# A graph network on one core: sorting the edges by block prefix counts and spreading the record scatters over later stages

## The reference

```python
h = relu(layernorm(x)); x = x + gat(relu(gat(h, W1, ...)), W2, ...)          # 0a and 0b: attention by dst
h = relu(layernorm(x)); x = x + dot_attention(h, Wq, Wk, Wv)                 # 1: by dst
h = relu(layernorm(x)); x = x + layernorm(segment_sum(
        silu(concat(h[src], edge_attr_64) @ W + b), dst))                    # 2: by dst, uses the edge attributes
h = relu(layernorm(x)); x = x + relu(segment_softmax_sum(h @ W, src, dst))   # 3: by src
```

## Time and profile before

| | us |
|---|---|
| median of 3 runs | 8227.57 (8222.74 to 8235.5) |
| the profiled execution | 8211.48 |
| its span | 8209.5 |
| setup | 86.2 |
| histogram | 142.3 |
| ranking | 1039.9 |
| units "d" | 107.4 |
| dense and scores 0a, 0b, 1, 2 | 446.3 together |
| dense and scores 3 | 119.7 |
| the four finish stages | 146.7 together |

### The profile page before, as it was taken

The page is one execution under the profiler, slowest core; times in us unless marked ns, Lnnn a source line. Parts: engine busy times, 40 slices in busy tenths (PEclk is TensorE's granted clock), DMA queues, the critical chain, the costliest instruction groups (busy, mean ns, idle before and its releaser), DMA issues. The chain is left out here.

```text
span 8209.5 us, 130687 instructions
## 1 busy us (share of the span) xinstructions
PE 5150.4 (63%) x21517; PEld 3732.5 (45%) x21518; DVE 5912.1 (72%) x16005; ACT 3435.3 (42%) x8014; POOL 4715.1 (57%) x4888
## 2 busy tenths in 40 slices
PE   1445551347777547777456767766688885577775
PEld 1344441235555335555344545544566663344443
DVE  4877774557777757777758888888566667577777
ACT  0122220057777347777324444443233331266664
POOL 0477773067777157777235555553477773377774
PEclk9999999998888668888788888887899997577777
DMA  4233332145455145555245555554344442254453
GB/s 157 76 102 102 104 104 49 46 127 135 135 135 135 34 121 135 135 135 134 45 136 166 166 166 166 166 166 117 97 128 128 128 128 63 82 135 135 135 135 93
DMA packets 608540, 981.03 MB, mean 119 GB/s; under 512 B 315833, under 2 KB 370550, under 8 KB 608026
## 3 DMA queue, kind: packets, MB, share of 16 engines
q0 software_dynamic: 248160, 655.67, 29.8%
q1 hardware_dynamic: 359898, 299.06, 12.8%
q10 hardware_dynamic: 416, 25.60, 0.9%
HBM read 945.69 MB, written 60.94 MB: 123 GB/s over the span
## 5 line engine op out<-in xcount | busy, mean ns | idle before, releaser
L1488 POOL DMA_INDIRECT ad_ring<-tab_qv,ad_idx x816 | 774.1, 949 | 946.6 <-PE ad_po L1690 278.2
L458 POOL DMA_INDIRECT recs_s<-plc_recr,plc_posu x784 | 774.3, 988 | 528.6 <-DVE plc_ohl L405 289.9
L1028 POOL DMA_INDIRECT at_ring<-tab_s,at_idx x816 | 784.0, 961 | 468.0 <-DVE acc L1041 216.0
L1028 POOL DMA_INDIRECT at_ring_0b<-tab_s,at_idx_0b x816 | 784.2, 961 | 455.7 <-issue 206.1
L1028 POOL DMA_INDIRECT at_ring_0a<-tab_s,at_idx_0a x816 | 784.9, 962 | 444.4 <-issue 210.0
L1879 POOL DMA_INDIRECT ae_ring<-tab_a,ae_idx x816 | 795.6, 975 | 397.0 <-issue 232.2
L438 PE MATMUL plc_got<-plc_base_sb,plc_lot 128*128 128x25 f32 x1568 | 488.4, 399 | 501.5 <-DVE plc_ohh L406 301.0
L438 PEld LDWEIGHTS plc_got<-plc_base_sb,plc_lot 128*128 128x128 f32 x1568 | 393.5, 312 | 593.4 <-issue 312.4
L1188 PE MATMUL at_po<-at_rows,at_hot 128*128 128x260 f32 x1632 | 563.4, 504 | 109.2 <-DVE at_begin L101 88.0
L1674 PE MATMUL ad_pk<-node_a,ad_hr 128*128 x1632 | 466.5, 436 | 235.3 <-DVE ad_prod L1547 132.3
L1188 PE MATMUL at_po_0a<-at_rows_0a,at_hot_0a 128*128 128x264 f32 x1632 | 512.4, 467 | 112.3 <-DVE at_begin_0a L101 87.2
(11 more groups left out here) (495 smaller groups left out, 13156.6 us busy)
## 6 DMA issues: line engine op xcount, KB each, us to landing
plc_krow<-keyrow_f SPq DMA_DIRECT2D x98, 512.0 KB
plc_lrow<-lorow_f SPq DMA_DIRECT2D x98, 512.0 KB
...
ae_feat<-attr_pad SPq DMA_DIRECT2D x816, 32.0 KB
...
```

What stands on the lines that cost most here:

```text
L458: eng.indirect_dma_start(out=order["s"]["recs"], out_offset=bass.IndirectOffsetOnAxis(ap=posu[:, k:k + 1], axis=0), in_=recr[:, k, :], in_ ...
L1028: eng.indirect_dma_start(out=ring[:, t.slot * STEP + u, :], out_offset=None, in_=table, in_offset=bass.IndirectOffsetOnAxis(ap=idx[:, t.sl ...
L1488: eng.indirect_dma_start(out=ring[:, t.slot * STEP + u, :], out_offset=None, in_=table, in_offset=bass.IndirectOffsetOnAxis(ap=idx[:, t.sl ...
```

## The change

The sort is written anew, and four fifths of its scatters leave it.

- `setup` no longer copies the attributes. ACT issues that DMA at the start of the histogram stage (now `cnt_`), with a semaphore `attr_copied` that nobody waits for until `aggregate_edges` (layer 2).
- The histogram stage works by blocks of 8 tiles. For tile k of a block PE adds the tile's counts to the prefix sums of all tiles from k on, in one matmul of (8 - k)·25 columns. ACT copies 7 of the 8 sums into `pre` (the counts before each tile of its block) and the last into `totals`. After the loop DVE makes a running sum over all blocks and from it `bases`, the first place of every key for each of the 98 blocks, which takes two memsets, a scan, a subtraction and an addition of 2450 columns each.
- The ranking stage (`rnk_`) takes a block in one step on each engine and works two blocks ahead. DVE makes `lot` (bf16) for block t+2 and `base` = `pre` + `bases`; ACT rounds it to bf16 (`high`), DVE keeps the remainder (`rest`). PE compares all pairs of a tile in one matmul whose right side also holds `high` and `rest`, together with a matmul that leaves only earlier edges above zero (`compare`); ACT copies that out through Relu (`keep`), and PE multiplies it with the one-hot of `hi` (`rank`). DVE picks the column and sums (`pick`, `place`, twice for 4 tiles each), then writes the places.
- Of the 8 tiles of a block, 2 (`SOON`) are scattered by POOL in this stage: 196 scatters. The places of the other 6 go to `edge_pos` in DRAM at the end (L434), their records to `edge_recs` at the start (L427, 12544 pieces of 96 bytes): 588 scatters left.
- A class `Scatter` loads a share of them in a later stage (SP, `feed`, ahead of the stage's other loads), issues the scatters (POOL, `send`) and waits for them (SP, `wait`) before the stage ends. The shares are: units "d" 72 (16 before its gathers, 56 behind them), dense 0a 84, finish 0a 28, dense 0b 72, finish 0b 32, dense 1 112, finish 1 20, dense 2 56, finish 2 40, dense 3 72.
- `units("s")` moves behind dense 3.

The diff, cut to its core:

```diff
-    @block.scalar
-    def _(eng):
-        eng.dma_start(attr_pad[0:E, :].rearrange("(a b) d -> a (b d)", a=16),
-                      attr_in.rearrange("(a b) d -> a (b d)", a=16)).then_inc(stored, 16)
...
+    for oh, digit, width in ((ohl[:, h, :, :], lo_e, P), (ohh[:, ts, :], hi_e, NB)):
...
+    st.own(eng, eng.memset(goes_on[:, :, :], 1.0))
+    st.own(eng, eng.memset(goes_on[:, :, 0:1], 0.0))
+    st.own(eng, eng.memset(pre[:, 0:T:HALF, :], 0.0))
+    eng.wait_ge(kept, 2 * BLOCKS + 4)
+    st.own(eng, eng.tensor_tensor_scan(
+        through[:, :, :].rearrange("p n b -> p (n b)"), goes_on[:, :, :].rearrange("p n b -> p (n b)"),
+        totals[:, :, :].rearrange("p n b -> p (n b)"), 0.0, ALU.mult, ALU.add))
+    st.own(eng, eng.tensor_copy(counts[:, :], through[:, :, BLOCKS - 1]))
...
+    st.own(eng, eng.tensor_tensor(through[:, :, :], through[:, :, :], totals[:, :, :], ALU.subtract))
+    st.own(eng, eng.tensor_tensor(
+        bases[:, :, :], through[:, :, :].rearrange("p n b -> p b n"),
+        start[:, :].rearrange("p (o n) -> p o n", o=1).to_broadcast([P, BLOCKS, NB]), ALU.add))
...
+    for k in range(HALF):
+        mm = eng.matmul(
+            sums[:, h, k * NB:HALF * NB].rearrange("p (k n) -> p k n", n=NB), ohl[:, h, k, :],
+            ohh[:, bass.ds(i * STEP + h * HALF + k, 1), :].to_broadcast([P, HALF - k, NB]),
+            start=(k == 0), stop=(k == HALF - 1), skip_group_check=True)
+    mm.then_inc(summed, 1)
...
+    eng.dma_start(attr_pad[0:E, :].rearrange("(a b) d -> a (b d)", a=16),
+                  attr_in.rearrange("(a b) d -> a (b d)", a=16)).then_inc(attr_copied, 16)
...
+    for h in range(2):
+        feed(turn(0, h))
+    eng.dma_start(edge_recs, rec_e[:, :, :].rearrange("p (b k) f -> p b k f", k=HALF)[:, :, SOON:HALF, :]
+                  .rearrange("p b k f -> p b (k f)")).then_inc(saved, 16)
+    with eng.Fori(0, LAST) as i:
+        for h in range(2):
+            eng.wait_ge(vec, v.at("lot", turn(i, h - 2)))
+            feed(turn(i, h + 2))
+    eng.wait_ge(vec, v.at("now", turn(LAST, 1)))
+    eng.dma_start(edge_pos, pos_rest[:, :, :].rearrange("p b k -> p (b k)")).then_inc(saved, 16)
...
+    def end(j):
...
+    eng.wait_ge(mat, m.at(f"rank{j}", t))
+    done(f"place{j}", t.plus(-1))
+    v.did(f"pick{j}", eng.tensor_tensor(
+        picked[:, j, :, :, :], got[:, t.slot, j, :, P:WB].rearrange("p t (k n) -> p t k n", k=2),
+        ohh[:, tile(t, j * HB, HB), :].rearrange("p t (o n) -> p t o n", o=1)
+        .to_broadcast([P, HB, 2, NB]), ALU.mult))
+    done(f"pick{j}", t)
+    v.did(f"place{j}", eng.tensor_reduce(
+        place[:, t.slot, subs(j)], picked[:, j, :, :, :].rearrange("p t k n -> p t (k n)"), AX.X,
+        ALU.add))
...
+    if begins:
+        eng.wait_ge(lrow_in[b.slot], b.lap * 16 + 16)
+        if ends:
+            eng.wait_ge(mat, m.at("compare1", t.plus(-1)))
+        v.did("lot", eng.tensor_scalar(both[:, b.slot, :, 0:P],
+                                       lrow[:, b.slot, :].rearrange("p (t e) -> p t e", e=P),
+                                       iota_col[:, :], None, ALU.is_equal))
+        v.did("base", eng.tensor_tensor(base[:, b.slot, :, :], pre[:, tile(b, 0, HALF), :],
+                                        bases[:, bass.ds(b.n, 1), :].to_broadcast([P, HALF, NB]),
+                                        ALU.add))
...
+    end(0)
+    if begins:
+        eng.wait_ge(act, a.at("high", t))
+        v.did("rest", eng.tensor_tensor(both[:, b.slot, :, P + NB:WB], base[:, b.slot, :, :],
+                                        both[:, b.slot, :, P:P + NB], ALU.subtract))
...
+    end(1)
+    if ends:
+        done("place1", t)
+        v.did("pos", eng.tensor_copy(pos_rest[:, bass.ds(t.n, 1), :].rearrange("p o k -> p (o k)"),
+                                     place[:, t.slot, SOON:HALF]))
+        eng.wait_ge(freed, t.n + 1)
+        v.did("now", eng.tensor_copy(pos_now[:, t.slot, :], place[:, t.slot, 0:SOON]))
...
+    eng.wait_ge(act, a.at("keep0", t.plus(-2)) if j == 0 else a.at("keep1", t.plus(-1)))
+    for k in range(HB):
+        mm = eng.matmul(got[:, t.slot, j, k, P + NB:WB], before[:, t.slot, j * HB + k, :],
+                        ohh[:, tile(t, j * HB + k, 1), :].rearrange("p o n -> p (o n)"),
+                        start=False, stop=(k % 2 == 1), skip_group_check=True)
+    m.did(f"rank{j}", mm)
...
+    eng.wait_ge(vec, v.at("rest", of.plus(-2)))
+    if free:
+        eng.wait_ge(vec, v.at(f"pick{j}", of.plus(-2)))
+    for k in range(0, HB, 2):
+        eng.matmul(got[:, of.slot, j, k:k + 2, 0:P], ident_b[:, :],
+                   not_later[:, :].rearrange("p (o e) -> p o e", o=1).to_broadcast([P, 2, P]),
+                   start=True, stop=False, skip_group_check=True)
+    for k in range(HB):
+        mm = eng.matmul(got[:, of.slot, j, k, 0:WB], both[:, of.slot, j * HB + k, 0:P],
+                        both[:, of.slot, j * HB + k, :], start=False, stop=False,
+                        skip_group_check=True)
+    m.did(f"compare{j}", mm)
...
+    rank(0)
+    compare(1, t.plus(1), not (first and t.k == -2) and (begins or t.k == 0), not first)
+    rank(1)
+    compare(0, t.plus(2), begins, not first)
...
+    eng.wait_ge(vec, v.at("base", t))
+    a.did("high", eng.activation(both[:, b.slot, :, P:P + NB], base[:, b.slot, :, :], ACT.Copy))
...
+    eng.wait_ge(mat, m.at("compare1", of.plus(-1)) if j else m.at("compare0", of.plus(-2)))
+    a.did(f"keep{j}", eng.activation(before[:, of.slot, subs(j), :], got[:, of.slot, j, :, 0:P],
+                                     ACT.Relu))
...
+    eng.wait_ge(freed, t.n + 1)
+    a.did("recs", eng.activation(recs_now[:, t.slot, :], rec_e[:, tile(t, 0, SOON), :]
+                                 .rearrange("p t f -> p (t f)"), ACT.Copy))
...
+    def scatter(t):
+        eng.wait_ge(act, a.at("recs", t))
+        eng.wait_ge(vec, v.at("now", t))
+        eng.sem_inc(told, 1)
+        for k in range(SOON):
             eng.indirect_dma_start(
                 out=order["s"]["recs"],
...
+    out_offset=bass.IndirectOffsetOnAxis(ap=pos_now[:, t.slot, k:k + 1], axis=0),
+    in_=recs_now[:, t.slot, 4 * k:4 * k + 4], in_offset=None).then_inc(landed[t.slot], 16)
...
+    with eng.Fori(0, LAST) as i:
+        for h in range(2):
+            eng.wait_ge(landed[h], i * (16 * SOON) + 16 * SOON)
+            eng.sem_inc(freed, 1)
+            scatter(turn(i, h + 2))
...
+    def feed(self, eng, n, slot):
+        at = self.first + n * self.count
+        eng.dma_start(self.recs[:, slot, :], edge_recs[:, bass.ds(at * 4, self.count * 4)]).then_inc(self.fed[slot], 16)
+        eng.dma_start(self.pos[:, slot, :], edge_pos[:, bass.ds(at, self.count)]).then_inc(self.fed[slot], 16)
+    def send(self, eng, lap, slot, which):
+        if which[0] == 0:
+            eng.wait_ge(self.fed[slot], lap * 32 + 32)
+            eng.sem_inc(self.told, 1)
+        for k in which:
+            eng.indirect_dma_start(
+                out=order["s"]["recs"], out_offset=bass.IndirectOffsetOnAxis(ap=self.pos[:, slot, k:k + 1], axis=0),
+                in_=self.recs[:, slot, 4 * k:4 * k + 4], in_offset=None).then_inc(self.landed[slot], 16)
+    def wait(self, eng, lap, slot):
+        eng.wait_ge(self.landed[slot], (lap + 1) * (16 * self.count))
...
     eng.iota(tio_i[:, :], [[1, T]], base=0, channel_multiplier=0).then_inc(iotas, 1)
+    if moving:
+        moving.send(eng, 0, 0, range(FIRST))
     eng.wait_ge(chain, marks["tuu"])
...
         eng.wait_ge(gathered, 16 * (j + 1))
+    if moving:
+        moving.send(eng, 0, 0, range(FIRST, scatter))
...
+    moving.send(eng, 0, 0, range(scatter))
...
     def _(eng):
+        if moving:
+            moving.feed(eng, 0, 0)
         for dst, src in w_ap:
             eng.dma_start(dst(W), src).then_inc(wl, 16)
...
+    if moving:
+        moving.wait(eng, 0, 0)
...
     eng.dma_start(We[:, :], we_ap).then_inc(wl, 16)
+    eng.wait_ge(attr_copied, 16)
     with eng.Fori(0, TURNS) as i:
...
-    units("d")
-    units("s")
+    units("d", 72)
-           stores=[(node_a, tab_s, TABW)])
+           stores=[(node_a, tab_s, TABW)], scatter=84 if norm else 72)
-        go(finish, tag, kind, [row(b)], 1e-16)
+        go(finish, tag, kind, [row(b)], 1e-16, scatter=28 if norm else 32)
-       b_aps=(bq, bv, bk), counted={1: 8}, stores=[(acc, tab_qv[:, 0:D], D), (acc_odd, tab_qv[:, D:2 * D + 8], D + 8)])
+       b_aps=(bq, bv, bk), counted={1: 8}, stores=[(acc, tab_qv[:, 0:D], D), (acc_odd, tab_qv[:, D:2 * D + 8], D + 8)], scatter=112)
-    go(finish, "1", "dot_add", [], 1e-16)
+    go(finish, "1", "dot_add", [], 1e-16, scatter=20)
-           b_aps=(L2b,), stores=[(node_a, tab_a, D)])
+           b_aps=(L2b,), stores=[(node_a, tab_a, D)], scatter=56)
-        go(finish, "2", "edge_add", [row(L2g), row(L2be)])
+        go(finish, "2", "edge_add", [row(L2g), row(L2be)], scatter=40)
-       scores=(L3as, L3an), gathered=1, stores=[(node_a, tab_s, TABW)])
```

(22 more changed lines are left out.)

423 lines of the change are left out of this document (222 added, 201 removed).

## The result

The changed kernel takes 7837.4 us (median of 4 runs, 7836.2 to 7838.7) for 8225.2 (4 runs, 8221.0 to 8235.5): ratio 0.953, 95% interval 0.951 to 0.954. It is faster by 388 us; the forecast was 661 (7566, range 7460 to 7700). The time missing is not in the ranking.

| part | forecast | measured |
|---|---|---|
| setup | -76 | 86.2 to 8.3: -77.9 |
| histogram, now count | +15 | 142.3 to 176.7: +34.4 |
| ranking | -692 | 1039.9 to 349.8: -690.2 |
| units d | +40 | 107.4 to 149.1: +41.8 |
| dense 0a, 0b, 1, 2, 3 | +13 | 575.8 to 592.5: +16.6 |

The account below looks back on a forecast made before the run. POOL's issue rate was taken to bound the ranking, an eighth of the span. Setup -76, histogram +15, ranking -692 and scatters in later stages +92 sum to -661, giving 7566 us, range 7460 to 7700.

Parts of the forecast that it names:

- Setup: Setup stage without the attribute copy: ends at 10 us for 86.2, -76, bounds -79 to -72.
- Ranking: Ranking stage: DVE sets the pace at 3.2 us per block, 348 us for 1040, -692.
- rival B: Ranking: PE at 1.2 GHz, in a chain DVE, PE, ACT, PE, DVE; a block takes 4.0 us, +78: 7644; chance 0.13.
- Count: Histogram stage: DVE's loop stays at 1.42 us per block, a new tail is added; +15, bounds 8 to 25.
- Units d: Units "d" stage: 56 scatters run behind its last gather, 147.6 us for 107.4, +40.
- dense: Dense 0a, 0b, 1, 2: own work covers nearly all scatters, 458.7 us for 446.3, +12; dense 3 costs 1.
- Finish: Four finish stages: DVE's long additions are shorter than POOL's list of 120 scatters, 184.9 us for 146.7, +38.
- rival C: Finish stages: scatters and DVE's 16 additions of 6.82 us hold each other up, +109: 7675; chance 0.10.

## Why the forecast was wrong

- **Setup** (-76): right, -77.9. The copy lies under the count: VectorE is busy 9.16 of 10 us with it (60 to 70 us, DMA share 1.02) and 9.20 without (140 to 150).
- **Ranking** (-692): the number right, -690, in part by luck, since its steps were off both ways. First scatter 21.6 us in (forecast 25), 3.28 a block ((570.03 - 252.15) / 97; forecast 3.2), end 10.2 (forecast 13). The text had VectorE as the bound, 3.19 us a block and near 90% busy; it is busy 2.61 us a block (256.15 / 98), 73%, and POOL 1.97. PE waits for VectorE's `rest` (L478), and VectorE for POOL to take the positions, so that the pace seems to be that of the chain through them and not of one engine. That is read from the waits and was not tested. It is rival B's chain, with a granted clock that does fall in this stage (0.67 on average), at 3.28 us and not at B's 4.0. Two waits of the ranking (total, times, longest):

```profile
PE rnk_got L518 <- DVE rnk_both L478: 93.6, 96, 8.0
DVE rnk_pos_now L488 <- POOLq L585: 29.9, 30, 2.7
```

`lot` took 0.50 us, between the row's 0.75 and the 0.38 that the prediction had by halving it. The Trainium skill ("VectorE: DVE Perf Modes", the perf-mode tier table) has 693 ns for bf16 against 1227 for f32 at 2048 elements, less than a factor of two; by that ratio 0.42 was to be expected, an estimate.
- **Count** (+15, measured +34.4): the mechanism of a loop bound by VectorE's pair, mis-sized. A pair takes 1.59 us ((209.7 - 53.8) / 98), not 1.42, mostly since VectorE waits for PE (0.13 a pair) and PE for ACT; the tail took 20.8, not 16, `bases`, read transposed, 4.7 of them.
- **Units d** (+40, measured +41.8) and **dense** (+13, measured +16.6): right. For dense it is helped by its base: the prediction took 446.3 us for the four stages, from windows that end with their last work, where they last 453.7 up to the next stage; its 458.7 for them after the change is 13 under the 472.0 measured.
- **Finish** (+38, measured +120.6): here rival C was right and my sum wrong. It said that scatters and the 16 additions of 6.82 us hold each other up; priced at 6.82 each it gave +109, by what was measured it is 16 x 5.6 = 90 and the shortfall is 83 (88 on the level, 272.4 for 184.9, as the base of 146.7 was 5 too small: finish 1 lasts 21.6 and not 16.4). I argued against it from the ranking, where the median scatter was within 5 ns of the shortest; but there no operation of VectorE is longer than 0.79 us, so that row could not show a wait for a long one. The Trainium skill ("GPSIMD Engine Reference", Key points) names contention with VectorE instructions in a two-port mode or with two SBUF inputs. The traces agree for two inputs: 6.5 to 6.9 us for a scatter of 0.96.
- **The stages that the change does not touch**: the step that failed most. The sum has no term for them, that is, 0, since their code is left alone. They cost 180 us: 158 in the attends, shown to be code fetched again, 30 in the aggregation, shown to hang on the place, less 8. The edit changed the VectorE instructions ahead of the loops and so moved the loops in memory. No rival named it. The Trainium skill has the rule ("Runtime: NRT & Kernel Launch", Instruction fetch mechanics): a taken branch whose target is no longer in an engine's instruction memory waits for a fetch. The trace agrees with that: 3.1 us per lap where the packets come, 0.24 where they don't. It differs on the block. The same section of the Trainium skill has 16 KiB, 256 instructions; here packets are 8192 bytes, and VectorE is 119 to 134 instructions further from one of the three within a lap to the next.

By the spans 286 us are missing: 188 in attends and aggregation, 83 in the finish stages, 19 in the count, and 4 less in all else. By the medians it is 273, since the span of before is 16 us under its median and that of after 3.
